# Attention scores from two fp32r parts in 48 rows, two heads in the two row halves of TensorE, in place of three bf16 parts in 96 rows

## The reference, cut to what matters

```python
q = (x @ Wq + bq).reshape(Bn, Nn, H, d)          # H = 16 heads, d = 16
k = (x @ Wk + bk).reshape(Bn, Nn, H, d)
v = (x @ Wv + bv).reshape(Bn, Nn, H, d)
scores = jnp.einsum('bnhd,bmhd->bnmh', q, k) / math.sqrt(d)
att = jax.nn.softmax(scores, axis=2)
attval = jnp.einsum('bnmh,bmhd->bnhd', att, v).reshape(Bn, Nn, Dn)
```

## Time and profile before

| | |
|---|---|
| runs of the kernel | 1202.48, 1202.98, 1203.63 us (median 1202.98) |
| profiled execution, span from first to last instruction | 1199.4 us |
| what lies around the span, as median minus span (the profiled execution has no time of its own beside its span) | 3.6 us |
| PE / PE weight loads / DVE / ACT / POOL busy | 1134.8 / 528.6 / 884.5 / 721.1 / 275.0 us |
| stages: prologue, units, mixture of experts and second layer | to about 117 us, to about 873 us, to the end |

### The profile page before, as it was taken

How to read it: one execution, slowest core, us unless ns; L and a number is a source line. 1 busy time by engine, 2 the same in 40 slices (tenths; PEclk the granted TensorE clock), 3 DMA queues, 4 the chain that set the end, 5 groups by cost and what they waited for, 6 DMA issues and landing times.

```text
span 1199.4 us, 18760 instructions
## 1 busy us (share of the span) xinstructions
PE 1134.8 (95%) x6130; PEld 528.6 (44%) x6130; DVE 884.5 (74%) x1113; ACT 721.1 (60%) x1279; POOL 275.0 (23%) x332
## 2 busy tenths in 40 slices
PE   5877999999999999999999999999999999999985
PEld 3442233333323333332333233233468778888874
DVE  5479888888878788787888888884666676656565
ACT  1523877777777778777777777777653232222321
POOL 2636772001001013010010000302230132312323
PEclk9989999999999999999999999998999999999996
DMA  7797000020000000000000000003010000000001
GB/s 161 174 135 153 1 15 14 1 75 2 14 15 1 14 15 1 14 10 6 15 1 14 15 1 15 1 1 122 1 53 1 18 1 1 19 1 15 4 0 35
DMA packets 33816, 34.53 MB, mean 29 GB/s; under 512 B 6640, under 2 KB 31184, under 8 KB 33744
## 3 DMA queue, kind: packets, MB, share of 16 engines
q1 hardware_dynamic: 30512, 31.90, 11.3%
q10 hardware_dynamic: 3232, 1.60, 0.7%
HBM read 24.70 MB, written 8.39 MB: 28 GB/s over the span
## 4 chain that ended last, share of the span: by engine, by line
PE 88%; DVE 3%; ACT 3%; DMA 3%; issue 1%; ACTq 1%; SPq 0%; POOL 0%; DVEq 0%; POOLq 0%
PE ps L555 21%; PE ps L533 20%; PE ps L493 19%; PE ps L691 12%; PE ps L679 7%; PE ps L433 1%; DMA bu<-su_b 1%; DMA kst<-k_parts 1%; DVE mxp L1239 1%; PE ps L619 1%; PE ps L850 1%; PE ps L444 1%; PE ps L821 1%; PE ps L905 1%; PE ps L597 1%
## 5 line engine op out<-in xcount | busy, mean ns | idle before, releaser
L1239 DVE TENSOR_REDUCE mxp<-ps 128x1 f32<-128x1024 f32 x512 | 602.9, 1220 | 147.2 <-PE ps L493 146.3
L1018 ACT ACTIVATE prob<-ps 128x512 f32<-128x512 f32 x1024 | 570.7, 597 | 148.4 <-PE ps L533 135.4
L533 PE MATMUL ps<-qst,kst 99*128 99x512 bf16 x1024 | 345.0, 386 | 6.4 <-issue 4.5
L493 PE MATMUL ps<-kst,qst 96*128 96x512 bf16 x1024 | 306.4, 382 | 21.4 <-DMA kst<-k_parts 9.4
L555 PE MATMUL ps<-prob,vp 128*32 128x512 f32 x2048 | 275.7, 611 | 0.0
L533 PEld LDWEIGHTS ps<-qst,kst 99*128 99x128 bf16 x1024 | 97.7, 97 | 297.3 <-ACT prob L1018 194.2
L493 PEld LDWEIGHTS ps<-kst,qst 96*128 96x128 bf16 x1024 | 98.1, 99 | 130.0 <-DVE mxp L1239 18.7
L1054 ACT ACTIVATE hid_hi<-hid 128x512 fp32r<-128x512 f32 (+1 forms) x56 | 35.4, 632 | 132.2 <-DVE hid L1391 102.9
L1739 POOL TENSOR_TENSOR att_u<-o_tm,rec 128x256 f32<-128x256 f32 x16 | 9.9, 619 | 376.6 <-DVE rec L1248 376.4
L555 PEld LDWEIGHTS ps<-prob,vp 128*32 128x32 f32 x2048 | 40.4, 108 | 108.5 <-issue 108.1
L1386 DVE SCALAR_TENSOR_TENSOR hid<-ps,bu,sig 128x512 f32<-128x512 f32 (+1 forms) x56 | 41.8, 747 | 48.8 <-PE ps L691 38.9
(11 more groups left out here) (218 smaller groups left out, 1116.0 us busy)
## 6 DMA issues: line engine op xcount, KB each, us to landing
qst<-q_parts SPq DMA_DIRECT2D x96, 64.0 KB, 2.3
kst<-k_parts SPq DMA_DIRECT2D x24, 256.0 KB, 13.2
k_parts<-kp SPq DMA_DIRECT2D x8, 384.0 KB, 2.6
q_parts<-qp SPq DMA_DIRECT2D x8, 384.0 KB, 4.3
x<-x SPq DMA_DIRECT2D x4, 512.0 KB, 9.4
wmod_sb<-wmod ACTq DMA_DIRECT2D x3, 512.0 KB, 8.7
wmod_sb<-wmod SPq DMA_DIRECT2D x1, 1536.0 KB, 6.3
out<-x SPq DMA_DIRECT2D x3, 512.0 KB, 2.9
```

What stands on the lines that cost most here:

```text
L493: last = nc.tensor.matmul(ps[:, 2 * p + m, :], qst[0:KR, g, hd, P * j:P * (j + 1)], kst[0:KR, G * g + hd, col:col + CH], start=True, stop= ...
L533: nc.tensor.matmul(ps[:, banks[n % len(banks)], :], kst[0:KR + NM, G * g + k, P * t:P * (t + 1)], qst[0:KR + NM, g, k, :], start=True, sto ...
L1018: nc.scalar.activation(prob[:, t % 2, k, :], ps[:, banks[(G * t + k) % len(banks)], :], ACT.Exp, scale=DH ** -0.5).then_inc(p_s, 1)
L1239: nc.vector.tensor_reduce(mxp[:, i, p:p + 1], ps[:, 2 * p:2 * p + 2, :], AX.XY, ALU.max).then_inc(mx_read, 1)
```

## The change

Query and key are split into two fp32r parts in place of three bf16 parts, and three products of parts are kept (`BLK` = 3, `NM` = 2). A head then needs 3 x 16 = 48 rows, and 50 with the two rows of the maximum. Head 2a lies in partitions 0 to 49, head 2a + 1 in partitions 64 to 113, and the matmuls of the two stand next to each other in the program, with outputs in two PSUM banks. `mxp` gets one column for each block of 512 keys, `nmp` two fp32r parts. One ACT rounding and one subtraction (on DVE straight from PSUM, for items 10 to 15 on POOL as before) make the two parts, in six slots (`parts`) that are stored and used again.

```diff
+HALF = 64
-BLK = 6
+BLK = 3
-NM = 3
-Q_PART = (0, 0, 1, 0, 2, 1)
-K_PART = (0, 1, 0, 2, 0, 1)
+NM = 2
+Q_PART = (0, 0, 1)
+K_PART = (0, 1, 0)
+HP = H // 2
+GP = G // 2
+SLOTS = 6
...
-        kst = at("kst", [P, H, T], BF16, k_reg)
-        qst = at("qst", [P, 4, G, CH], BF16, q_reg)
+        kst = at("kst", [P, HP, T], F32R, k_reg)
+        qst = at("qst", [P, 4, GP, CH], F32R, q_reg)
...
             def project(n, ks=range(2)):
-                    if n >= 2:
-                        pe.wait_ge(q32_s, n - 1)
+                    if n - 2 >= EASY:
+                        pe.wait_ge(q32_s, n - 1 - EASY)
+                    elif n >= 2:
+                        pe.wait_ge(lo_s, n - 1)
...
             def maxima(g, i, p, n):
-                hd, j = i // TPC, i % TPC
-                for m in range(2):
-                    col = CH * (2 * p + m)
-                    last = nc.tensor.matmul(ps[:, 2 * p + m, :], qst[0:KR, g, hd, P * j:P * (j + 1)],
-                                            kst[0:KR, G * g + hd, col:col + CH], start=True, stop=True)
+                a, j, m = i // (2 * TPC), i // 2 % TPC, 2 * (i % 2) + p
+                for b in range(2):
+                    rows = slice(HALF * b, HALF * b + KR)
+                    last = nc.tensor.matmul(ps[:, 2 * p + b, :], qst[rows, g, a, P * j:P * (j + 1)],
+                                            kst[rows, GP * g + a, CH * m:CH * (m + 1)], start=True, stop=True)
...
             def unit(u, g, ahead, first=False, beside=None, banks=(4, 5, 6)):
-                    for k in range(G):
-                        n = G * t + k
...
+                    for a in range(GP):
+                        n = G * t + 2 * a
+                        two_banks = [banks[(n + b) % len(banks)] for b in range(2)]
+                        turn_max = a == 1 and t == TURN_MAX and ahead >= 1
                         if turn_max:
                             pe.wait_ge(p_s, u * (G * MT) + n - len(banks) + 1)
+                            max_row(u + 1, two_banks[0])
                             pe.wait_ge(nmT_s, u + 2)
-                        if n >= len(banks):
-                            pe.wait_ge(p_s, u * (G * MT) + n - len(banks) + 1)
+                        if n + 1 >= len(banks):
+                            pe.wait_ge(p_s, u * (G * MT) + n + 1 - len(banks) + 1)
...
+                        for b in range(2):
+                            rows = slice(HALF * b, HALF * b + KR + NM)
+                            last = nc.tensor.matmul(ps[:, two_banks[b], :], kst[rows, GP * g + a, P * t:P * (t + 1)],
+                                                    qst[rows, g, a, :], start=True, stop=True)
+                        last.then_inc(sc_ps, 1)
+                        if run and not late:
+                            maxima(vg, i, a, pairs + a)
...
             def item(n):
-                nc.scalar.activation(parts_of(n)[:, 0], ps[:, 4 + n % 2, :], ACT.Identity, bias=bias)
-                nc.scalar.activation(q32[:, n % 2, :], ps[:, 4 + n % 2, :], ACT.Identity, bias=bias).then_inc(q32_s, 1)
+                nc.scalar.activation(halves_of(n)[:, 0], ps[:, 4 + n % 2, :], ACT.Identity, bias=bias).then_inc(hi_s, 1)
+                if n >= EASY:
+                    nc.scalar.activation(q32[:, n % 2, :], ps[:, 4 + n % 2, :], ACT.Identity, bias=bias).then_inc(q32_s, 1)
...
                     for k in range(G):
-                        if k == 1 and t == TURN_MAX and ahead >= 1:
+                        if k == 2 and t == TURN_MAX and ahead >= 1:
                             max_rows(u + 1, banks[(G * t + k) % len(banks)])
-                        act.wait_ge(sc_ps, u * (G * MT) + G * t + k + 1)
+                        if k % 2 == 0:
+                            act.wait_ge(sc_ps, u * (GP * MT) + GP * t + k // 2 + 1)
...
             def residue(n):
-                nc.vector.tensor_tensor(res[:, n % 2, :], q32[:, n % 2, :], hi, ALU.subtract).then_inc(r_s, 1)
+                nc.vector.scalar_tensor_tensor(both[:, 1], ps[:, 4 + n % 2, :], bias, both[:, 0].bitcast(F32),
+                                               ALU.add, ALU.subtract).then_inc(lo_s, 1)
...
             def reduce_pair(i, p, n):
-                nc.vector.tensor_reduce(mxp[:, i, p:p + 1], ps[:, 2 * p:2 * p + 2, :], AX.XY, ALU.max).then_inc(mx_read, 1)
+                nc.vector.tensor_reduce(own, ps[:, 2 * p:2 * p + 2, :], AX.X, ALU.max).then_inc(mx_read, 1)
...
             def split_max(v):
                 nc.gpsimd.tensor_copy(nmp[:, 0, :], nm32[:]).then_inc(nm_step, 1)
...
-                nc.gpsimd.tensor_tensor(nmp[:, 2, :], nmr[:], nmp[:, 1, :], ALU.subtract).then_inc(nm_s, 1)
+                nc.gpsimd.tensor_tensor(nmp[:, 1, :], nm32[:], nmp[:, 0, :].bitcast(F32), ALU.subtract).then_inc(nm_s, 1)
```

More of the change, by code:

```diff
@@ L316, in load_gate_up @@
+            def store_max(slot):
+                for b in range(2):
+                    for m in range(NM):
+                        row = HALF * b + KR + m
+                        sp.dma_start(qst[row:row + 1, slot, :, :].bitcast(F32).rearrange("p k (j n) -> p (k j) n", j=TPC),
+                                     nmp[MI // 2 * b:MI // 2 * (b + 1), m, :].bitcast(F32)).then_inc(nm_in, 16)
             def load_gate_up(dst, experts, shared, sem_):
@@ L519, in unit @@
                         if turn_max:
                             pe.wait_ge(p_s, u * (G * MT) + n - len(banks) + 1)
-                            max_row(u + 1, banks[n % len(banks)])
-                        for p in range(2):
-                            if run and place[p] == k:
-                                if late and p == 0:
-                                    pe.wait_ge(oT_s, u)
-                                maxima(vg, i, p, pairs + p)
-                        if turn_max:
+                            max_row(u + 1, two_banks[0])
@@ L536, in unit @@
+                        last.then_inc(sc_ps, 1)
+                        if run and not late:
+                            maxima(vg, i, a, pairs + a)
+                    if run and late:
+                        pe.wait_ge(oT_s, u)
+                        for p in range(2):
+                            maxima(vg, i, p, pairs + p)
                     if t == 0 and not first:
```

197 lines of the change are left out of this document (86 added, 111 removed).

## The result

The changed kernel took 1256.41 us (median of four runs, 1248.15 to 1261.1) against 1203.31 us of the kernel before on the same chip (four runs, 1202.48 to 1203.98): a ratio of 1.0439, 95% interval 1.0401 to 1.0477. The forecast was 1234 us, with a range of 1172 to 1300.

The account below looks back on a forecast made before the run. PE's stream was taken to bound the kernel. Loop steps +21, other steps with maxima +2, step 12 +10, unit 14's last steps +1, prologue -3: +31 on 1199.4, plus 3.6, gives 1234 us; range 1172 to 1300, own range 1208 to 1258.

Parts of the forecast that it names:

- the step: One loop step becomes a chain through ACT's first exponential and the second score pair: 2.95 us against 2.84.
- W: The weighing on PE, four float32 matmuls in column strips, queued behind the second pair's wait: 1.00 us, unchanged.
- The lag of the second half: Second matmul of a pair starts 0.01 us after the first, taken from the column strips.
- the load's term: fp32r weight load that nothing covers: 0.11 us, paid twice a step, at the first and second score pairs.
- queued loads: Rival, 17%: each pair's lag is a whole weight load, 0.11 us; +47 us, giving 1281, up to 1300.
- no concurrency: Rival, 7%: the two row halves don't run together; 0.68 us more a step, +160 us, giving 1394.
- loads ahead of the wait: Rival, 17%: weight loads are done before the wait, both 0.11 vanish; loop step 2.73 us, giving 1182.
- The whole gain: Rival, 3%: PE loses four of eight matmul times and DVE sets 2.44 us a step; -94 us, about 1109.
- the prologue's bounds: Work ahead of the units, with third projection waiting for DVE but keys split sooner: -3 us, bounds -8 and +2.
- step 12: Step with ACT's copy of the maxima: two exponentials now precede the copy, 3.77 us, 0.72 more than before.
- the clock as all or nothing: Rival, 10%: PE's rest in each step drops the clock to 1.2 GHz; +400 us if it stays, +200 at half.
- PEclk leaves 1.00 inside the units: Sign that the forecast is wrong: PE's granted clock falls below full inside the units.

Follow-up runs that it names:

- The bf16 run: Changed kernel with scores and maxima reading only the upper two bytes of each number as bf16, pairs, rows and waits kept; output inexact: 1188.79 us, one run.
- the run in one half: Changed kernel with both matmuls of each pair reading the same row half, so they cannot run together; output wrong: 1974.33 us, one run.
- the paired bf16 kernel: Kernel before, three bf16 parts in 96 rows, with only the changed kernel's pair waits and place of the maxima: 1270.68 us, one run.
- split pair: Changed kernel with the second score pair taken apart: third head at once, then W, then fourth head alone behind the exponential: 1214.55 us, 1.0117 of the kernel before.
- all edits without idle matmuls: Changed kernel with split pair, W in step 12's wait for the turned maxima and PE's loop written out: 1187.38 us, 0.9863 of the kernel before.

## Why the prediction was right, and where its sizes were off

**Right: the step.** Forecast 2.95, measured 2.93, and each link: exponential 0.62 after the pair (forecast 0.62), second pair 0.65 on, W 0.67 on (0.68), W itself 0.99 (1.00). The lag of the second half is nothing that the records show (0.01). The bf16 run confirms the load's term, the run in one half the pairing, the paired bf16 kernel the wait. Rivals out: queued loads (0.70 to the exponential), no concurrency (0.85), loads ahead of the wait (0.50); the timeline has 0.62. The whole gain is out as well: DVE waits 0.44 in each step.

**The rest, part by part.** Profiled spans, changed kernel less kernel before:

| part | forecast | measured |
|---|---|---|
| up to the first exponential | -3 | +10.7 |
| from there to the first output copy (unit 0) | +1.3 | +6.2 |
| units 1 to 13, longer steps | +30.9 | +25.4 |
| units 1 to 13, what is left, at the loop edges | 0 | +11.5 |
| units 14 and 15 | +2.4 | +4.2 |
| after the last output copy | 0 | -2.1 |
| sum | +31.6 (+31 as rounded there) | +55.9 |

So the direction and the mechanism were right and the size was short by 24 us. The prologue, unit 0 and the loop edges added 30 more than the forecast had for them, and the steps, less long than forecast, took 5.5 back. The stated range of 1172 to 1300 held with ease; it is wide because it takes in two rivals that did not come true. The forecast's own range, 1208 to 1258, held by 2 us, and with luck: 0.04 a step on 235 steps and the prologue's bounds give only 1220 to 1248, which does not hold the result.

**Mis-sized: the units' sum.** The forecast gave 2.46 to a loop unit; measured at full clock are 1.95. The step has 0.09 and not 0.11, and step 12 has 0.57 more than before and not 0.72:

```profile
720.88 0.50 PE L546 MATMUL ps<-qst,kst 50*128 50x512 f32 x2
...
722.47 0.25 ACT L981 ACTIVATE nm<-ps 16x128 f32<-16x128 f32 x1
...
722.85 0.49 PE L546 MATMUL ps<-qst,kst 50*128 50x512 f32 x2 [1.03 <-ACT nm L981]
...
724.50 0.50 PE L546 MATMUL ps<-qst,kst 50*128 50x512 f32 x2
```

From pair to pair 3.62 (3.05 in the earlier trace rows; forecast 3.77), the second pair 1.97 after the first and not 2.09.

**Mis-sized: the prologue, forecast -3, profiled +10.7 at the first exponential.** PE took up the third projection at 29.10, as the prediction's order of DVE said (2 us late). But then its eight matmuls took 6.36 us in place of some 3.7, at the lower clock:

```profile
29.10 6.36 PE L450 MATMUL ps<-hT,wk_sb 128*128 128x512 f32 x8 [4.25 <-DVE parts L1208]
...
66.03 0.79 PE L510 MATMUL ps<-kst,qst 48*128 48x512 f32 x2 [6.04 <-DMA kst<-k_parts]
```

The last key item was ready for its store at 46.8 us, 1.1 later than before and not 1.3 earlier, the first maxima began at 66.03 and not at 64.73, and PE went through them and the projections beside them at the lower clock from 66 to 88 us, 96% busy, where the kernel before was up at 68. Most of the 10.7 is chance, though. The runs hold three more profiles of the changed kernel's prologue, unaltered, and their first exponentials are at 121.8 (loop written out), 123.8 (split pair) and 124.7 us (all edits without idle matmuls). Two more of the kernel before's (paired bf16, loop written out) have 122.3 both. Taken by the middle of each, the prologue costs about 2 us, the upper bound that the prediction gave, and the profile shown here is the longest of the seven.

**Mis-sized: the clock as all or nothing.** I gave it 10% at +200 to +400. It was neither: the units hold full clock although PE rests 0.54 in each step, and each episode costs 0.36 of its length. The price of a step at the lower level was right (4.6 forecast, 4.58 measured); what was missing was a stretch that begins and ends. The prediction named "PEclk leaves 1.00 inside the units" as a sign of being wrong, and that sign came, behind both loop edges. Behind the edges the changed kernel spends 34 us at the lower level and the kernel before 3: 31 x 0.36 = 11 us, which is the table's row. Around the start of unit 0 it is 20 us for 7: 13 x 0.36 = 5 us, the excess of that row. The changed kernel's four runs line up with the clock: 1248.15, 1255.76, 1257.07 and 1261.1 us at a mean clock of 0.958, 0.951, 0.950 and 0.944.

**Open.** Why the clock comes back within 5 us after a pause in the kernel before and after 20 in the changed one. It is not the rest in each step alone: the paired bf16 kernel, which rests too, paused 2.28 us up to 378.15 and was at full clock again by 385:

```profile
385.00:390.00 5.00, 4.88 (x29) 1.24 (x28) 3.65 (x4) 3.08 (x7) 0.00 (x0) 1.00 0.00 0
```

Behind the same edge the bf16 pairs of 50 rows in two halves were at the lower level for less than 15 us (0.50 from 350 to 360, 1.00 from 365). The runs show which streams are slow to come back (pairs of 48 to 50 rows, in fp32r more than in bf16), not what decides it. In the changed kernel the second edge cost less than the first (10 us at the lower level for 24), and no run says why.

## What to carry to other kernels

Pairing two instructions also pairs their waits. Before halving an engine's work, write down from the timeline the loop start, handover, buffer free, and see whether the pair's second buffer puts another engine's latency in front of everything queued behind it; here 0.9 us of matmul time in a step was bought with a wait of 0.54 and two open weight loads. Keep together what is free at the same time, let the late one wait alone, and put the longest independent work (W) ahead of that wait. And a pause of 2.4 us that costs 3 in one kernel can cost 9 in another (6 and 17 us for the two loop edges here): count the stretch behind it in the windows, at the lower clock's price. Before you give a difference in a prologue to the change, look at the same instructions in a second execution: here they differed by 9 us.

## What the runs showed of the hardware that was not expected

- Two fp32r matmuls of 50 rows in the two row halves of TensorE start together: 0.50 us for both, the record of one.
- With both in one half PE was 99% busy from 200 to 1500 us and the granted clock averaged 0.51 there; in the kernel before it was 1.00 at 99% busy, and with PE at 81% in the changed kernel with its loop written out 1.00 over 650 us. Busy time in the records alone does not tell the clock.
- After a pause of 2.38 us the changed kernel stayed at the lower clock for over 20 us, the kernel before for less than 10 after 2.08 and not at all after 2.40 (PEclk 1.00 from 543 to 550 us).
- With matmuls whose result nobody reads, put where PE waits, the clock of the split-pair kernels was 1.00 from 115 to 135 us in three profiles (0.66 in the two without them); in the changed kernel it fell all the same (0.51 from 120 to 142).
